# Last batch's values behind its scores, exponentials before the gelus, a finer grid for threshold counts, last tile in five banks

## The reference

```python
# L1 attention (per token, over the 16 heads), then its experts
qkv = x @ w_qkv + b_qkv                       # q, k, v: 16 heads of 64
k = k + pos_enc[None, :, None, :]
attn = softmax(einsum('blhd,blgd->blhg', q, k) / 8)
out = einsum('blhg,blgd->blhd', attn, v).reshape(B, L, 1024) @ w_out + b_out

probs = softmax(xt @ Wg)                      # 2048 tokens, 8 experts
_, top_idx = top_k(probs.T, 256)              # each expert takes its 256 best tokens
# tok2exp: the best expert that took the token, else the token's best expert
for e in range(8):
    gate = where(tok2exp == e, weights, 0)
    out = out + gate[:, None] * (gelu(xt @ W1[e], approximate=False) @ W2[e])
```

## Time and profile before

| | |
|---|---|
| time, median of 3 runs | 807.25 us (806.21 to 807.82) |
| the profiled execution | 807.88 us, of it span 805.8 us |
| mean granted TensorE clock | 0.989 |
| PE busy | 760.5 us, 94% of the span |
| DVE, ACT, POOL busy | 547.0, 404.5 and 182.4 us |

### The profile page before, as it was taken

One profiled execution on the slowest core, in us unless ns is written; L12 is line 12 of the kernel. 1 busy time (PEld: TensorE's weight loads), 2 busy tenths in 40 slices (PEclk: granted clock), 3 DMA queues, 4 the chain that ended last, 5 costly groups with the idle time before them and its releaser, 6 DMA issues.

```text
span 805.8 us, 16963 instructions
## 1 busy us (share of the span) xinstructions
PE 760.5 (94%) x6585; PEld 577.1 (72%) x6585; DVE 547.0 (68%) x1639; ACT 404.5 (50%) x1105; POOL 182.4 (23%) x232
## 2 busy tenths in 40 slices
PE   3889999999999999999999999999999878999994
PEld 2765765874877588658766876687587757999984
DVE  5548837769666876677677868677859453255695
ACT  1665535355535654564456435623651466554563
POOL 1132113062115301530252034204302231000000
PEclk9999999999999999999999999999999998999998
DMA  8922002302040204020311212030204340000000
GB/s 238 343 70 53 1 2 54 89 18 54 2 106 1 54 2 106 2 53 24 84 27 28 59 49 53 2 87 20 54 2 106 106 106 1 1 1 2 8 21 26
DMA packets 53989, 42.57 MB, mean 53 GB/s; under 512 B 37852, under 2 KB 46700, under 8 KB 52504
## 3 DMA queue, kind: packets, MB, share of 16 engines
q1 hardware_dynamic: 53912, 41.51, 19.4%
HBM read 31.93 MB, written 9.58 MB: 52 GB/s over the span
## 4 chain that ended last, share of the span: by engine, by line
PE 85%; DVE 5%; ACT 4%; issue 2%; DMA 2%; POOL 1%; SPq 0%; ACTq 0%; DVEq 0%
PE ps L1491 13%; PE ps L1567 12%; PE ps L1599 7%; PE ps L1705 6%; PE ps L1693 6%; PE ps L1586 4%; PE ps L1654 4%; PE ps L1669 4%; PE ps L1477 4%; PE ps L1499 3%; PE ps L1521 3%; PE ps L1510 2%; PE ps L1450 2%; PE ps L1617 2%; PE ps L1426 2%
## 5 line engine op out<-in xcount | busy, mean ns | idle before, releaser
L1491 PE MATMUL ps<-veF,hB 128*128 128x512 f32 x256 | 121.4, 606 | 0.0
L1108 DVE COPY_PREDICATED shared<-ghot,ps 128x512 f32<-128x512 int32 x128 | 88.0, 725 | 3.3 <-PE ps L1491 0.6
L715 ACT ACTIVATE sc<-sc,nmax 128x128 f32<-128x128 f32 (+1 forms) x128 | 57.2, 447 | 59.4 <-DVE nmax L1094 59.4
L1491 PEld LDWEIGHTS ps<-veF,hB 128*128 128x128 f32 x256 | 45.3, 189 | 49.9 <-issue 40.2
L535 POOL TENSOR_TENSOR sc<-sc,rg 128x384 f32<-128x384 f32 x64 | 51.6, 827 | 69.8 <-DVE rg L1081 69.8
L1693 PE MATMUL ps<-hE,veF 128*128 128x256 f32 x256 | 59.5, 384 | 4.7 <-ACT early_masks L810 2.3
L1567 PE MATMUL ps<-early_masks,oeF 128*128 128x256 f32 x256 | 62.9, 385 | 0.5 <-issue 0.5
L527 POOL TENSOR_TENSOR sc<-sc,rdenA 128x512 f32<-128x512 f32 x32 | 32.5, 1040 | 133.5 <-DVE rdenA L1035 133.5
L1567 PE MATMUL ps<-wide,oeF 128*128 128x256 f32 x256 | 62.3, 386 | 0.0
L1599 PE MATMUL ps<-hC,early 128*64 128x128 f32 x1024 | 60.3, 275 | 1.6 <-ACT hC L636 1.6
L1599 PEld LDWEIGHTS ps<-hC,early 128*64 128x64 f32 x1024 | 55.5, 137 | 6.2 <-issue 4.3
(11 more groups left out here) (233 smaller groups left out, 1559.0 us busy)
## 6 DMA issues: line engine op xcount, KB each, us to landing
chosen<-hot_scratch SPq DMA_DIRECT2D x16, 512.0 KB, 5.8
v_scratch<-shared SPq DMA_DIRECT2D x16, 512.0 KB, 5.1
vg<-v_scratch SPq DMA_DIRECT2D x16, 512.0 KB, 5.5
veF<-in_L_ffn_value_experts SPq DMA_DIRECT2D x1, 2048.0 KB, 10.2
oeF<-in_L_ffn_output_experts SPq DMA_DIRECT2D x1, 2048.0 KB, 14.6
early<-in_L_attn_w_qkv SPq DMA_DIRECT2D x1, 1536.0 KB, 17.8
shared<-bias_scratch SPq DMA_DIRECT2D x2, 512.0 KB, 6.8
veF<-in_L_ffn_W SPq DMA_DIRECT2D x1, 1024.0 KB, 5.3
```

The source lines that it names most:

```text
L715: act.activation(v, v, ACT.Exp, bias=nmax[:, h % RING, t:t + 1], scale=-1.0, accum_out=denB[:, h * T + t:h * T + t + 1]).then_inc(s_("f_e" ...
L1108: dve.copy_predicated(val[:, t, :].rearrange("p (h k) -> p h k", h=HF), ghot[:, t * HF:(t + 1) * HF, e].bitcast(I32).unsqueeze(2) .broadca ...
L1491: pe.matmul(ps[:, vbank(j), :], tok(hB, t), veF[:, :].rearrange("p (h e k) -> p e h k", h=HF, e=EF)[:, e, :, :], start=True, stop=True).th ...
```

## The change

Four edits in one.

1. Batch 7's four value matmuls stand behind its scores (inside `last_softmax`) and not ahead of them, in banks 1, 2, 3 and 4; `hidden(0)` takes banks 5, 6, 7, 1, 2, 3, 5, 6. DVE's four `evac_v` follow its maxima. The logits of batch 6 move with the values.
2. ACT does the four exponentials first, then the logits' exponentials, then all gelus of batch 0.
3. The stream of the experts has 32 places to a batch (two in each hidden expert). The 15 counts stand every fifth place from place 21 of batch 1, the three later steps 3, 5 and 10 places behind the last. The DVE loop is written out; in the first 11 steps the candidates come from `many` directly. `PROBS` of batch 7 moves from behind expert 6 to behind expert 7 of `hidden(1)`.
4. ACT's `weigh` is gone: DVE weights all kept batches; `ENDS` is 0, 1, 2, 5, 3, 4, 6, 7. The last tile goes to banks 6, 6, 7, 7, 1, 1, 2, 3, and DVE sums its experts one by one behind PE; its output has a transfer of its own.

The tables of `in_order` and of the end:

```diff
-            in_front_last = {"qk0": (PROJECT,), "qk2": (ADD,), "qk4": (NORM,), "qk6": (MODULATE,), "v": (LOGITS,),
-                             "s": (PROBS,)}
-            in_experts = {(0, 17): (PROJECT,), (0, 20): (ADD,), (0, 21): (NORM,), (1, 2): (MODULATE,), (1, 4): (LOGITS,),
-                          (1, 6): (PROBS,)}
+            in_softmax_last = {"v": (LOGITS,), "probs": (PROBS,)}
+            in_experts = {(0, 25): (PROJECT,), (0, 28): (ADD,), (0, 29): (NORM,), (1, 5): (MODULATE,), (1, 9): (LOGITS,),
+                          (1, 15): (PROBS,)}
...
-        ENDS = ((0, "W"), (1, "W"), (5, "D"), (2, "S"), (6, "D"), (3, "S"), (4, "S"), (7, "D"))
+        ENDS = (0, 1, 2, 5, 3, 4, 6, 7)
+        LAST_BANKS = (6, 6, 7, 7, 1, 1, 2, 3)
```

On ACT:

```diff
-            def last_softmax(b, k, n):
-                inner(0, 0)
-                inner(0, 1)
-                exponent(b, 0)
-                inner(0, 2)
-                inner(0, 3)
-                exponent(b, 1)
...
+            def last_softmax(b, beside):
+                for q in range(QUARTERS):
+                    exponent(b, q)
+                beside("v")
+                for e in range(E1):
+                    inner(0, e)
                 keep(0, 0)
                 keep(0, 1)
```

On DVE:

```diff
-            def last_softmax(b, k, n):
+            def last_softmax(b, beside):
                 for q in range(QUARTERS):
                     add(b, q)
                     greatest(b, q)
+                beside("v")
+                evac_v(b, 0)
+                evac_v(b, 1)
                 for q in range(QUARTERS):
                     total(b, q)
+                beside("probs")
...
-            with dve.Fori(0, STEPS * (KEPT - 2)) as i:
+            for i in range(STEPS * (KEPT - 2)):
...
+                if i < EXACT:
+                    dve.tensor_tensor(base[:, :], bits[:, i * 3 + 3:i * 3 + 6], thr[:, :].broadcast_to([P, 3]),
+                                      ALU.bitwise_or).then_inc(s_("r_base"), 1)
+                    dve.wait_ge(s_("r_base"), i + 1)
                 dve.wait_ge(s_("r_sum"), i + 1)
                 dve.tensor_scalar(reached[:, :], ps[:, 0, P:P + 3], float(CAP), 0.0, ALU.is_ge, ALU.add,
                                   accum_out=many[:, :]).then_inc(s_("r_many"), 1)
                 dve.wait_ge(s_("r_many"), i + 1)
+                if i < EXACT:
+                    dve.scalar_tensor_tensor(out=cand[:, :], in0=many[:, :].broadcast_to([P, 3]), scalar=place(i),
+                                             in1=base[:, :], op0=ALU.mult, op1=ALU.add).then_inc(s_("r_cand"), 1)
...
+            def last_tile():
+                sum_ = eprod[:, T - 1, 0:D]
+                for e in range(E1):
+                    dve.wait_ge(s_("e_last"), e + 1)
...
+                        dve.scalar_tensor_tensor(out=sum_, in0=y, scalar=w, in1=sum_, op0=ALU.mult,
+                                                 op1=ALU.add).then_inc(s_("e_sum"), 1)
```

On PE:

```diff
+            def project_v(b, t):
+                for i in (2 * t, 2 * t + 1):
+                    if values1_bank(b, i) == 4 and i > 0:
+                        pe.wait_ge(s_("c_sc"), b * QUARTERS + 1)
+                    pe.matmul(ps[:, values1_bank(b, i), :], tok(hV, t), wqkv1[:, (i % 2) * 8:(i % 2 + 1) * 8, 2, :],
+                              start=True, stop=True).then_inc(s_("c_v"), 1)
...
             def hidden(b, beside):
                 for e in range(E1):
-                    pe.wait_ge(s_("e_g"), b * E1 + (e - 1 if e >= 3 else 1))
+                    if b > 0:
+                        pe.wait_ge(s_("e_g"), b * E1 + (e - 1 if e >= 3 else 1))
+                    elif e < 3:
+                        pe.wait_ge(s_("c_sc"), (B - 1) * QUARTERS + e + 2)
+                    elif e < 6:
+                        pe.wait_ge(s_("c_vs"), (B - 1) * 4 + e - 2)
+                    else:
+                        pe.wait_ge(s_("e_g"), e - 4)
...
-            def last_softmax(b, k, n):
+            def last_softmax(b, beside):
+                project_v(b, 0)
+                beside("v")
+                project_v(b, 1)
                 loaded(pe, "experts")
                 pe.wait_ge(s_("h_kept"), 2)
                 hidden(0, alone)
-                pe.wait_ge(s_("c_sc"), B * QUARTERS)
+                beside("probs")
                 outer(0, 0, alone)
...
-            counts = ((1, 14), (1, 20), (2, 1), (2, 4), (2, 7), (2, 13), (2, 19), (3, 1), (3, 4), (3, 7), (3, 13), (3, 19),
-                      (4, 1), (4, 4), (4, 7))
+            counts = [slot_of(FIRST_SLOT + SLOTS_A_STEP * i) for i in range(STEPS * (KEPT - 2))]
```

More of the change, by code:

```diff
@@ L201, in adaln_kernel @@
         many = sb("many", [P, 1])
+        base = sb("base", [P, 3], I32)
         rm = sb("rm", [P, 3, P])
@@ L602, in _ @@
             for b in range(2):
-                for place in range(3 * E1):
-                    beside((b, place))
+                for slot in range(SLOTS):
+                    beside((b, slot))
         @block.scalar
@@ L846, in _ @@
                 for e in range(E1):
+                    beside((b, 2 * e))
                     inner(b, e)
-                    beside((b, e))
-                for place in range(E1, 3 * E1):
-                    beside((b, place))
+                    beside((b, 2 * e + 1))
+                for slot in range(2 * E1, SLOTS):
+                    beside((b, slot))
                 if b < KEPT:
```

208 lines of the change are left out of this document (118 added, 90 removed).

## The result

The changed kernel takes **793.89 us** (median of 4 runs, 791.55 to 795.16), the kernel before 807.13 on the same chip (806.21 to 807.82): ratio 0.9835, 95% interval 0.9813 to 0.9857, so 13.2 us faster. It was run again with the last experiments: 793.20 us, ratio 0.9812 (0.9797 to 0.9827). The forecast was 796.4 us with a range of 792.0 to 800.5. The profiled execution took 793.85 us, with a span of 791.8 us (805.8 before).

A forecast was written before the change was run, and what follows sets the result against it. PE was taken as the bound, carrying 85% of the chain, with losses in the last softmax, expert stream and end. -6.8 + 1.4 - 0.43 + 0.5 - 0.67 - 4.85 = -10.85 from 807.25 gives 796.4 us, range 792.0 to 800.5.

The forecast's parts named there:

- rival A: Last softmax: the relay makes PE wait but the clock stays up, 1.4 us less, 795.0 us; chance 0.25.
- The matmul side of the softmax: Last softmax: scores start 3.3 us earlier, PE is never held before 664.9, back1 could start 9.5 us earlier.
- The relay's wait: Ahead of back1: waiting for the relayed values, a new 2.7 us wait; back1 starts 6.8 us earlier, not 9.5.
- rival B: Last softmax: the relay is not late, back1 starts at 666.3 and no clock is lost, 792.3 us; chance 0.12.
- The clock: Behind PE's 3.2 us idle ahead of back1: the granted clock falls and costs 1.4 us (0 to 1.6).
- The counts: Expert stream: 14 steps take 33.9 us without PE waiting; behind the last count a wait of +0.5 us (0 to 0.9).
- Rivals C and D: Threshold steps: PE waits 0.40 us in each of 14, 802.0 us, chance 0.12; or straight code slower than before, chance 0.04.
- PROBS and batch 6: Expert stream: two PE waits go, -0.43 us for the logits' exponentials and -0.67 us at batch 6's first outer.
- The weighting: Late expert stream: DVE's extra weighting frees batch 6's banks at 779.1, PE wants them at 780.9, covered by 1.8 us.
- The end: Behind PE's last matmul: DVE ends 3.4 us later and not 8.24, -4.85 us (-5.5 to -4.2).
- The last transfer: Final output store: half the bytes, counted as nothing (0 to -0.3 us).

The follow-up runs named there:

- warm: The changed kernel with four matmuls that nobody reads added on TensorE in the relay's wait ahead of back1; 790.51 us, ratio 0.981 against the kernel before.
- experiment 3: The changed kernel with the count matmuls and the three later steps back at their old places; 801.74 us, ratio 0.9961 against the kernel before.
- old_ends: The changed kernel with the old end: VectorE's old order, ScalarE weighting kept batches 2, 3, 4, standard banks, one store; 797.34 us, ratio 0.9874.
- direct_last: The changed kernel with the last tile in the two standard banks, weighted like other tiles, keeping its own store; 792.83 us, ratio 0.9836.
- experiment 8: The kernel before, unchanged, run and profiled once more; 806.41 us.
- v_ahead: The changed kernel with batch 7's value matmuls and batch 6's logits put back ahead of the scores; 792.12 us, ratio 0.9837 against the kernel before.

## Why the prediction was right

The forecast lies 2.5 us above the median, inside its range. The median lies below the band that was called likeliest (794.8 to 798) and nearer to rival A (795.0) than to the forecast; that it is not A is shown by the trace alone, where the clock fell. The mechanisms that the sum was built on are in the trace; most of the sizes came out longer than they are, one (the end) shorter, and 1.7 us of the 14.0 are luck (the last two points).

- **The matmul side of the softmax** came as worked out: `outer` was forecast to end at 664.9 and ended at 664.4, with 0.6 us of that from the earlier start, and one table load stands before the first gelu. The 9.5 us that this was to give were counted from a `back1` that half clock had made 1.3 us late in the one execution that was read; the prediction named the half clock at 664 to 668 us and not that at 672 to 676.
- **The relay's wait** that takes the place of the slow softmax is there: TensorE idles 2.09 us ahead of `back1`, forecast 3.2. The mis-sized term is the relay: 12.6 us from the first write to the last landing (13.0 from rows 5, less 0.4), and it took 11.6. The Trainium skill's "DMA: Bandwidth & Descriptors", section "Anatomy of one DMA", which the prediction set beside rival B with an estimate of 3.2 us a transfer, gives its figures for transfers that GpSimd issues, and these are SyncE's; the rows have 4.6 and 5.3 us, so the trace does not agree with it here either.
- **The clock**: +1.4 forecast, +1.43 measured, and `warm` shows it. Rival A remained possible in any one execution: the fall came in seven of eight. The Trainium skill's "TensorE: Matmul & The Clock Gate", Part 1, has the point at which the clock rises at a kernel's start differ from run to run; here it is the fall that does.
- **The counts**: 33.9 us for 14 steps, forecast and measured; behind the last count +0.37 against +0.5. Rivals C and D did not come. The 2.82 us that the prediction took for VectorE's own need in a step held 0.55 us of waiting for TensorE's sum, besides the 0.40 of the loop; that it was left with just the 2.42 us of five places was chance, and VectorE had more room than it gave it. After the change VectorE waits 0.90 us for the sum in a step, of which the sum itself needs a part.
- **PROBS and batch 6**: the waits went, -0.70 and -0.91 against -0.43 and -0.67. The difference is a term that was not in the sum. The first row behind a wait is longer (1.13 for 0.86 us, 7.38 for 7.14), mostly because the first matmul's whole length counts there, while in an unbroken row it overlaps with the one before: four such matmuls at 683.70 last 1.03 us too, and the next starts 0.86 us behind them. That part goes with the wait.
- **The weighting** that VectorE takes over from ScalarE was to be covered by 1.8 us; the trace has 1.6 (776.90 against 778.50). The sentence carried more than it says: without the finer grid the cover is gone, and TensorE pays 10.0 us (experiment 3).
- **The end**: -4.20 against -4.85. The eight operations start 0.45 us apart and not 0.37, the upper end of what was bounded. The sum was nearly right, but it ran the parts together: the gain is that of the order and of VectorE's weighting in ScalarE's place (distance of `old_ends` +4.7, of `direct_last` -0.7 on the changed kernel's), and the five banks on which the step dwelt cost 0.55 us.
- **The last transfer** was counted at nothing, with 0.3 as an end, and gave 1.43. Of it 0.3 is its size and 1.1 goes with the instruction packet beside the last store of the kernel before (experiment 8). No part of the change aimed at that and the prediction does not have it: luck.
- **0.6 us** came from the scatter of the code ahead, as an execution's luck.

## What to carry to other kernels

Undo parts one by one and in pairs: of five parts one (the exponentials together) carried the softmax, two (grid and order) were worth 4.9 us together, nothing (the grid) and -5 us (the order) apart, and two (the values behind the scores, the five banks) nothing. Where TensorE waits for a transfer of some 2 us, give it work that is needed anyway, or any: behind the wait the clock cost 1.4 us more. Read the kernel before in two executions, or a half clock that only one of them has is booked as the change's gain. An early result helps only if an engine is free to take it; ask which one before giving it a bank.

## What was not expected of the hardware

- TensorE idle for 1.92 to 2.19 us ahead of `back1` was followed by a fall to the level of 1.2 GHz in seven of eight executions (granted clock 0.55 and 0.59 from 668 to 672 us in the changed kernel), and cost 1.2 to 1.5 us each time. Waits of 0.4 to 1.3 us in `v_ahead` were followed by none. In the kernel before, the last `outer` matmuls waited 2.26 us in one execution and 2.14 in the other; the first was followed by half clock, the second was not.
- Eight dependent operations of 128x128 out of PSUM on VectorE start 0.45 us apart (0.36 busy, the rest wait and issue); ScalarE's copies with a scale from the same banks take 0.31 us each.
- With an instruction packet beside it a store of 128 KB was late in 23 of 33 cases, by up to 1.8 us (3.60 for 1.82), and without one in none of 70. The last store of the kernel before took 2.95 and 2.66 us.
- The same code ahead of the change ended anywhere between 644.55 and 648.70 us in the profiled executions, more than most parts of the change are worth. A distance inside the trace told them apart where the medians did not.
